# Mixture of experts behind attention: tokens fetched by indirect DMA instead of one-hot products

## The chip, the cores and the metric

The kernel runs on one core of a Trainium2 chip. The time is the device time of one execution, in microseconds (us); the figure given for a kernel is the median of its runs. Inside the core there are five engines with their own queues: TensorE (PE, with its weight loads shown as PEld), VectorE (DVE), ScalarE (ACT), GpSimd (POOL) and SyncE (SP, which here issues DMAs). They wait for one another through semaphores only.

## The reference

One pre-norm layer on x of 16 batches, 256 tokens, 128 features, all float32.

```
x = x + attention(layernorm(x))            # 16 heads, key width 8, value width 64, causal
n = layernorm(x)
probs = softmax(n @ gate_w)                # 8 experts
top_p, top_idx = top_k(probs per expert and batch, 64)      # each expert takes 64 of the 256 tokens
xin = n[top_idx]                           # (batch, expert, 64, 128)
h = gelu(xin @ w1[expert])                 # 128 -> 512
y = (h @ w2[expert]) * top_p               # 512 -> 128
x = x + scatter_add(y at top_idx)
```

## The kernel before

**Attention (lines 83 to 692).** One block. Every engine walks the same schedule of batches and, in each batch, of four units (four heads each); later stages of a batch run one to three batches behind the first. The second layer norm of batch b - 2 is made by DVE in unit 0 of batch b (`norm(xn2, ...)`, line 507) into one buffer xn2, which PE transposes in unit 1 for the gate product (line 614). In unit 1 ACT also copies xn2 to `xg_hi` (line 434, rounded to the matmul type float32r), and in unit 2 DVE writes `xg_lo`, what the rounding left (line 530). Both are kept for all 16 batches. SP stores and reloads q and k through DRAM for each batch (from line 257), loads w1 at batch 4 and w2 near the end.

**Routing (lines 871 to 911).** A second block begins when every engine has left the first. DVE makes the softmax, PE transposes it so that a row is one pair of batch and expert, and DVE finds the 64 largest of 256 in eight rounds. `tok_row` (the indices as bfloat16) goes to DRAM and comes back spread over all partitions, two batches to a load (`toks`, line 805). The indices and the probabilities are also transposed into `slot_tok` and `slot_prob`: partition = slot of an expert pair, column = batch. Meanwhile ACT and POOL split w1 into w1_hi and w1_lo (lines 838, 823).

**Experts (from line 941 on DVE, 991 on PE).** The loop `for n in STEPS` runs over -4 to 17. A step n is one pair of experts (n mod 4) for one group of four batches (n // 4), so 16 steps have products. In its step each engine does, in this order:

- PE: the pick of batch n + 4, the h products of step n (24 products: two halves of two experts, each as hi x hi, hi x lo, lo x hi), the out product of batch n - 5, the y products of step n - 1 (64 products).
- DVE: `picks(n + 5)`, which compares `toks` with the token numbers and gives a one-hot matrix; the copy of `xin_lo`; `add_out(n - 5)`, which adds two halves of the out product to x_all; `placing(n - 3)`, four one-hot matrices that put the slots back to token rows; the scaling of y by the probabilities.
- ACT: the copy of `xin_hi`, four Gelus with the rounded copy of y (`split_y`, step n - 2) between the second and the third.
- POOL: the low part of y (line 828), one pass for each step.

A pick is four products of 512 columns: xg_hi and xg_lo of a batch's two token blocks, each times the one-hot matrix. It gives the 64 tokens of all eight experts, feature by slot, so that four picks serve four steps; four of them stand ahead of the first h product. Out products of the last four batches stand behind the loop and write where the picks wrote; `last_place` reuses the pick matrices.

What the prediction's steps touch: lines 434 and 530 (xg), 507 (xn2 and its wait), 800 to 805 (the trip of the indices), 823 and 828 (POOL), 852 and 947 (xin), 863 (Gelu), 909 (slots), 926 (places), 977 (out), 999 (pick), 1018 to 1020 (h), 1035 (y).

Of the kernel before, what the change touches and what calls it, by code (L numbers as in the profile page):

```python
# [5 lines left out]
F32 = mybir.dt.float32  # L6
# [47 lines left out]
def block_kernel(nc, x, w_q, w_k, w_v, w_o, gate_w, w1, w2, out):  # L54
# [3 lines left out]
    with ExitStack() as ctx:  # L58
        def sb(name, shape, dt=F32, scope=ctx):
            return scope.enter_context(nc.sbuf_tensor(name, shape, dt))  # L60

        def sem(name, scope=ctx):
            return scope.enter_context(nc.semaphore(name))


        x_all = sb("x_all", [P, B * TB, D])
        xg_hi = sb("xg_hi", [P, B * TB, D], F32R)
        xg_lo = sb("xg_lo", [P, B * TB, D], F32R)
# [6 lines left out]
        experts_loaded = sem("experts_loaded")  # L75

        attention(nc, x_tiles, w_q, w_k, w_v, w_o, gate_w, w1, w2,
                  x_all, xg_hi, xg_lo, gate_logit, ident, w1_raw, w2_sb, k_diag_even, experts_loaded)
        experts(nc, out_tiles, x_all, xg_hi, xg_lo, gate_logit, ident, w1_raw, w2_sb,
                experts_loaded)  # L80


def attention(nc, x_tiles, w_q, w_k, w_v, w_o, gate_w, w1, w2,
              x_all, xg_hi, xg_lo, gate_logit, ident, w1_raw, w2_sb, k_diag_even, experts_loaded):
# [4 lines left out]
    with ExitStack() as ctx:  # L89
# [118 lines left out]
        xg_hi_done = sem("xg_hi_done")  # L208
        xg_lo_done = sem("xg_lo_done")
# [28 lines left out]
        def _(sp):  # L238
# [127 lines left out]
        def _(act):  # L366
# [23 lines left out]
            def batch(b, par):  # L390
                for j in range(G):
# [40 lines left out]
                    if j == 1 and has(b - 2, B):  # L432
                        act.wait_ge(xn2_ready, b - 1)
                        nc.scalar.activation(xg_hi[:, bass.ds((b - 2) * TB, TB), :], xn2[:, :, :],
                                             ACT.Copy).then_inc(xg_hi_done, 1)
# [4 lines left out]
        def _(dve):  # L440
# [26 lines left out]
            def batch(b, par):  # L467
                for j in range(G):
# [58 lines left out]
                    if j == 2 and has(b - 2, B):  # L527
                        dve.wait_ge(xg_hi_done, b - 1)
                        tiles = bass.ds((b - 2) * TB, TB)
                        nc.vector.tensor_tensor(xg_lo[:, tiles, :], xn2[:, :, :], f32(xg_hi[:, tiles, :]),  # L530
                                                ALU.subtract).then_inc(xg_lo_done, 1)
# [164 lines left out]
def experts(nc, out_tiles, x_all, xg_hi, xg_lo, gate_logit, ident, w1_raw, w2_sb, experts_loaded):  # L696
# [5 lines left out]
    with ExitStack() as ctx:  # L702
# [6 lines left out]
        def sem(name):  # L709
# [5 lines left out]
        LB = 2  # L715
        LOADS = B // LB
        STEPS = range(-4, B + 2)
# [12 lines left out]
        tok_row = sb("tok_row", [P, CAP], BF16)  # L730
# [4 lines left out]
        tok_no = sb("tok_no", [P, TB])  # L735
        col_no = sb("col_no", [P, T], BF16)
        toks = [sb(f"toks{r}", [P, LB, E * CAP], BF16) for r in range(RING)]
        pick = [sb(f"pick{r}", [P, TB, E * CAP], F32R) for r in range(RING)]
        xin_hi = [sb(f"xin_hi{r}", [P, E, QB, CAP], F32R) for r in range(RING)]
        xin_lo = [sb(f"xin_lo{r}", [P, E, QB, CAP], F32R) for r in range(RING)]  # L740
# [4 lines left out]
        place = [sb(f"place{r}", [P, EP, T], F32R) for r in range(RING)]  # L745
        tok_rows = nc.dram_tensor("tok_rows", [P, CAP], BF16).ap()

        pick_hi_ps = [ps(f"pick_hi_ps{r}", [P, E, CAP]) for r in range(RING)]
        pick_lo_ps = [ps(f"pick_lo_ps{r}", [P, E, CAP]) for r in range(RING)]
# [3 lines left out]
        last_place = [part[:, :, :].rearrange("p t (a n) -> p (t a) n", a=2) for part in pick]  # L753
        last_out_ps = [to[:, :, :].rearrange("p (t a e) s -> p t a (e s)", t=TB, a=2)
                       for to in (*pick_hi_ps, *pick_lo_ps)]

        def out_ps_of(b):

            return out_ps[:, :, :, :] if b < LAST else last_out_ps[b - LAST]

        def place_of(b):

            return place[b % RING][:, :, :] if b < B - RING else last_place[b % RING]
# [7 lines left out]
        row_ready = sem("row_ready")  # L771
        row_stored = sem("row_stored")
        toks_loaded = [sem(f"toks_loaded{i}") for i in range(LOADS)]
# [5 lines left out]
        pick_ready = sem("pick_ready")  # L779
        pick_done = sem("pick_done")  # L780
# [17 lines left out]
        def _(sp):  # L798
            sp.wait_ge(row_ready, 1)
            sp.dma_start(tok_rows, tok_row[:, :]).then_inc(row_stored, 16)  # L800
            sp.wait_ge(row_stored, 16)
            rows = tok_rows.rearrange("(b e) s -> b (e s)", e=E)
            for i in range(LOADS):
                await_count(sp, pick_ready, (i - 1) * LB)
                sp.dma_start(toks[i % RING][:, :, :],
                             bcast(rows[i * LB:(i + 1) * LB, :], 0, P)).then_inc(toks_loaded[i], 16)
# [6 lines left out]
        def _(pool):  # L813
            nc.gpsimd.iota(tok_no[:, :], pattern=[[P, TB]], base=0, channel_multiplier=1,
# [5 lines left out]
            for ep in range(EP):  # L820
# [3 lines left out]
                                        ALU.subtract).then_inc(w1_ready, 1)  # L824
            for m in range(B):
# [3 lines left out]
                                        f32(parts[:, :, m % EP, 0, :]), ALU.subtract).then_inc(y_lo_ready, 1)  # L829

        @block.scalar
        def _(act):
# [14 lines left out]
            for n in STEPS:  # L847
                b = n + 4
                if has(b, B):
                    act.wait_ge(pick_done, b + 1)  # L850
                    await_count(act, h_done, (b // QB - 1) * 16)
                    nc.scalar.activation(xin_hi[b // QB % RING][:, :, b % QB, :], pick_hi_ps[b % RING][:, :, :],  # L852
                                         ACT.Copy).then_inc(xin_hi_ready, 1)
# [11 lines left out]
                elif has(m, B):  # L865
                    split_y(m)

        @block.vector
        def _(dve):
# [30 lines left out]
            nc.vector.tensor_copy(tok_row[:, :], at).then_inc(row_ready, 1)  # L900
# [10 lines left out]

            def picks(b):

                if has(b, B):
                    if b % LB == 0:
                        dve.wait_ge(toks_loaded[b // LB], 16)
                    await_count(dve, pick_done, b - 1)
                    for tb in range(TB):
                        last = nc.vector.tensor_scalar(pick[b % RING][:, tb, :], toks[b // LB % RING][:, b % LB, :],  # L919
                                                       tok_no[:, tb:tb + 1], None, ALU.is_equal)  # L920
                    last.then_inc(pick_ready, 1)
# [18 lines left out]
            picks(0)  # L940
            for n in STEPS:
                picks(n + 5)
                b = n + 4
                if has(b, B):
                    dve.wait_ge(pick_done, b + 1)
                    await_count(dve, h_done, (b // QB - 1) * 16)
                    nc.vector.tensor_copy(xin_lo[b // QB % RING][:, :, b % QB, :], pick_lo_ps[b % RING][:, :, :]).then_inc(xin_lo_ready, 1)
# [8 lines left out]
                if B - RING <= b < B:  # L956
                    dve.wait_ge(pick_done, B)
                    placing(b)
                m = n - 1
# [12 lines left out]
        def _(pe):  # L972
# [18 lines left out]
            for n in STEPS:  # L991
                b = n + 4
                if has(b, B):
                    pe.wait_ge(pick_ready, b + 1)
                    await_count(pe, xin_hi_ready, b - 1)
                    await_count(pe, xin_lo_ready, b - 1)
                    for part, to in ((xg_hi, pick_hi_ps[b % RING]), (xg_lo, pick_lo_ps[b % RING])):
                        for tb in range(TB):
                            last = nc.tensor.matmul(to[:, :, :], part[:, b * TB + tb, :], pick[b % RING][:, tb, :],  # L999
                                                    start=(tb == 0), stop=(tb == TB - 1))  # L1000
                    last.then_inc(pick_done, 1)
                if has(n, B):
# [4 lines left out]
                    quarter = n // QB  # L1007
                    pe.wait_ge(xin_hi_ready, (quarter + 1) * QB)
                    pe.wait_ge(xin_lo_ready, (quarter + 1) * QB)
                    for k in range(4):  # L1010
                        e = 2 * (n % EP) + k // 2
                        await_count(pe, h_ready, 4 * n + k - 1)
                        for c in range(2):
                            hidden = slice((2 * (k % 2) + c) * P, (2 * (k % 2) + c + 1) * P)
                            xh = xin_hi[quarter % RING][:, e, :, :].rearrange("p b s -> p (b s)")
# [54 lines left out]
```

## Time and profile before

| | |
|---|---|
| median of 3 runs | 591.7 us (591.56 to 592.28) |
| profiled execution | 592.4 us |
| its span | 590.7 us |
| mean granted clock of TensorE | 0.976 of full speed |
| PE busy | 533.6 us, 90% |
| DVE, ACT, POOL busy | 403.1, 403.0, 252.3 us |
| DMA | 45.82 MB |

The span is the time from the first to the last instruction in the profile; 1.7 us of the profiled execution lie around it. Busy times overlap one another. Matmuls are pipelined: one is shown for longer than the distance to the next, so that the distance between starts says what a product costs in a row. The granted clock is a share of 2.4 GHz.

### The profile page before, as it was taken

Reading aid. Unit: us, or ns where it says so; the run is one execution under the profiler, and the core shown is the slowest. Engines: PE = TensorE matmul, PEld = TensorE weight load, DVE = VectorE, ACT = ScalarE, POOL = GpSimd, SP = SyncE. Lnnn points to the kernel's source line nnn. Section 1 sums busy time; section 2 is a strip of 40 time slices with the busy share of each in tenths; the row PEclk is TensorE's granted clock in tenths of the full one; section 3 lists DMA queues with packets and bytes.
Section 4 is the critical chain, followed back from the end, with each engine's and each line's share of the span. In section 5 each row is a group of like instructions: output and inputs, shape, how many; then the busy total and the mean of one; then the engine's idle time right before and its main releaser. Section 6 shows DMA issues by size and latency. Waiting matters only on the chain. (4 is left out here: it accounts for less than half of the span.)

```text
span 590.7 us, 14103 instructions
## 1 busy us (share of the span) xinstructions
PE 533.6 (90%) x4773; PEld 429.9 (73%) x4773; DVE 403.1 (68%) x1014; ACT 403.0 (68%) x1378; POOL 252.3 (43%) x245
## 2 busy tenths in 40 slices
PE   1599999999999999999999999997059999999996
PEld 1367777777777777777777777776038989989895
DVE  1477888888888888888888887874863234433344
ACT  4698988989889889888888898971215443243230
POOL 4155565555565555555655555560600110110111
PEclk9999999999999999999999999999569999999999
DMA  4585142652251431522513315500020001000001
GB/s 116 159 221 146 33 121 74 214 144 71 74 142 32 110 98 44 142 71 71 143 40 102 112 33 140 144 1 1 1 67 24 20 19 37 20 11 19 19 20 46
DMA packets 49739, 45.82 MB, mean 78 GB/s; under 512 B 4256, under 2 KB 46496, under 8 KB 49696
## 3 DMA queue, kind: packets, MB, share of 16 engines
q1 hardware_dynamic: 48832, 44.60, 27.6%
q10 hardware_dynamic: 864, 0.66, 0.4%
q8 instruction: 26, 0.43, 0.3%
q14 instruction: 17, 0.14, 0.1%
HBM read 26.35 MB, written 18.89 MB: 77 GB/s over the span
## 5 line engine op out<-in xcount | busy, mean ns | idle before, releaser
L385 ACT ACTIVATE prob<-s_ps,neg_max 128x128 f32<-128x128 f32 (+1 forms) x512 | 210.2, 437 | 21.7 <-DVE neg_max L542 20.1
L358 POOL TENSOR_TENSOR probn<-prob,inv 128x1024 f32<-128x1024 f32 x64 | 121.2, 1894 | 45.6 <-DVE inv L546 45.6
L385 ACT ACTIVATION_READ_ACCUMULATOR prob<-s_ps,neg_max 128x1 f32 x512 | 113.9, 223 | 0.0
L351 POOL TENSOR_TENSOR probn<-prob,inv 128x512 f32<-128x512 f32 x64 | 66.6, 1041 | 87.7 <-PE t_ps L659 79.3
L637 PE MATMUL ctx_ps<-probT,v_sb 128*64 128x256 f32 (+1 forms) x1024 | 97.3, 332 | 0.6 <-issue 0.6
L637 PEld LDWEIGHTS ctx_ps<-probT,v_sb 128*64 128x64 f32 x1024 | 63.5, 136 | 27.7 <-issue 9.1
L828 POOL TENSOR_TENSOR y_parts<-y_sb,y_parts 128x512 fp32r<-128x512 f32 x16 | 20.5, 1284 | 137.1 <-ACT y_parts L844 137.1
L473 DVE TENSOR_REDUCE neg_max<-s_ps 128x4 f32<-128x1024 f32 x64 | 76.5, 1196 | 1.3 <-PE s_ps L575 1.3
L650 PE MATMUL misc_ps<-wo_sb,ctxT 128*128 128x128 f32 x512 | 73.9, 288 | 0.0
L650 PEld LDWEIGHTS misc_ps<-wo_sb,ctxT 128*128 128x128 f32 x512 | 61.9, 191 | 10.8 <-issue 10.8
L599 PE MATMUL t_ps<-ident,probn 128*128 128x128 f32 x256 | 62.9, 286 | 1.0 <-ACT probT L423 0.7
L600 PE MATMUL t_ps<-ident,probn 128*128 128x128 f32 x256 | 60.2, 275 | 0.0
L1035 PE MATMUL y_ps<-w_sb,w_raw 128*64 128x128 f32 x1024 | 59.4, 274 | 0.0
L539 DVE COPY probT<-t_ps 128x512 f32<-128x512 f32 x64 | 44.2, 690 | 21.6 <-PE t_ps L659 21.5
L852 ACT ACTIVATE xin_hi<-pick_hi_ps 128x512 fp32r<-128x512 f32 x16 | 9.6, 599 | 71.9 <-PE pick_lo_ps L999 71.9
L542 DVE TENSOR_REDUCE neg_max<-s_ps 128x4 f32<-128x512 f32 x64 | 44.3, 692 | 19.1 <-PE s_ps L690 18.9
L1035 PEld LDWEIGHTS y_ps<-w_sb,w_raw 128*64 128x64 f32 x1024 | 55.6, 137 | 2.1
L863 ACT ACTIVATE w_raw<-h_ps 128x512 f32<-128x512 f32 x64 | 38.2, 599 | 26.0 <-PE h_ps L1020 23.7
L430 ACT ACTIVATE v_sb<-misc_ps 128x512 f32<-128x512 f32 x64 | 38.3, 599 | 24.7 <-PE misc_ps L557 23.7
L535 DVE COPY ctxT<-ctx_ps 128x512 f32<-128x512 f32 x64 | 43.6, 682 | 4.8 <-PE ctx_ps L637 4.8
L485 DVE CAST s_ps<-causal 128x512 f32<-128x512 bf16 x63 | 42.4, 674 | 0.0
L423 ACT ACTIVATE probT<-t_ps 128x512 f32<-128x512 f32 x64 | 41.5, 648 | 0.4 <-PE t_ps L600 0.4
(146 smaller groups left out, 1044.5 us busy)
## 6 DMA issues: line engine op xcount, KB each, us to landing
qT<-q_rows SPq DMA_DIRECT2D x15, 512.0 KB, 4.0
q_rows<-qk_hi SPq DMA_DIRECT2D x32, 128.0 KB, 2.4
q_rows<-qk_lo SPq DMA_DIRECT2D x32, 128.0 KB, 2.4
k_diag_odd<-k_rows SPq DMA_DIRECT2D x32, 128.0 KB, 4.3
k_rows<-qk_hi SPq DMA_DIRECT2D x30, 128.0 KB, 2.4
k_rows<-qk_lo SPq DMA_DIRECT2D x30, 128.0 KB, 2.4
k_diag_even<-k_rows SPq DMA_DIRECT2D x28, 128.0 KB, 4.3
w_raw<-in_L_ffn_w SPq DMA_DIRECT2D x1, 2048.0 KB, 10.4
```

Of the source, the lines that this page charges most:

```text
L351: nc.gpsimd.tensor_tensor(probn[r][:, 0:HG * P].rearrange("p (i k) -> p i k", i=HG), prob[r][:, 0:HG * P].rearrange("p (i k) -> p i k", i=HG),
L358: nc.gpsimd.tensor_tensor(probn[r][:, HG * P:].rearrange("p (i k) -> p i k", i=HG), prob[r][:, HG * P:].rearrange("p (i k) -> p i k", i=HG ...
L385: last = nc.scalar.activation(prob[r][:, first + i * keys:first + (i + 1) * keys], scores[:, i, :], ACT.Exp, bias=neg_max[:, r, block_, i: ...
L473: nc.vector.tensor_reduce(out=neg_max[:, r1, 1, :], in_=s1_ps[:, :, :], axis=AX.X, op=ALU.max, negate=True).then_inc(max1, 1)
L535: nc.vector.tensor_copy(ctxT[r2][:, :, :], ctx_ps[:, :, :]).then_inc(ctx_ready, 1)
L539: nc.vector.tensor_copy(probT[rm][:, 1024:1536], t_ps[rm][:, :]).then_inc(t_dve, 1)
L542: nc.vector.tensor_reduce(out=neg_max[:, r2, 0, :], in_=s0_ps[:, :, :], axis=AX.X, op=ALU.max, negate=True).then_inc(max0, 1)
L599: nc.tensor.transpose(t[:, i, 0:P], q0[:, 2 * f + i, :], ident[:, :])
L600: last = nc.tensor.transpose(t[:, i, P:T], q1[:, 2 * f + i, 0:P], ident[:, :])
L637: last = nc.tensor.matmul(ctx_ps[half * DV:(half + 1) * DV, pair, kb * P:T], v_sb[vb][:, kb, h * DV:(h + 1) * DV], rhs, start=(kb == 0), s ...
L650: last = nc.tensor.matmul(misc_ps[1][:, tb * D:(tb + 1) * D], ctxT[rm][:, c, tb * P:(tb + 1) * P], wo_sb[:, 2 * g + c, :], start=(g == 0 a ...
L1035: last = nc.tensor.matmul(y_ps[half * CAP:(half + 1) * CAP, q, :], hT[m % RING][:, half, c, q * CAP:(q + 1) * CAP], w2_sb[:, 2 * (m % EP) ...
```

## The change

The one-hot pick is replaced by a fetch from DRAM. In attention SP stores xn2 of each batch to a DRAM tensor `xn2_rows` (256 rows of 512 bytes a batch), and DVE waits for that store before it overwrites xn2; xg_hi and xg_lo are gone. The trip of the indices is gone as well. In its place DVE adds the batch's first row number to slot_tok (`slot_row`, unsigned integers), and POOL issues, for each step, four indirect DMAs, one for each batch of the group: row p of the buffer `xs` gets the DRAM row whose number stands in partition p of `slot_row`. There are five such buffers, so five steps are issued ahead, and from then on four gathers follow each low part of y. PE transposes the four 128 x 128 blocks of a step into one PSUM bank (`xin_ps`), one step ahead, behind the h and out products and ahead of the y products. ACT copies it to xin_hi; DVE then writes xin_lo as the difference, which needs xin_hi first. The loop starts at -1 instead of -4.

```
     sync, attention
+    def store_tokens(b):
+        sp.wait_ge(xn2_ready, b + 1)
+        sp.dma_start(xn2_rows[b * T:(b + 1) * T, :].rearrange("(t p) d -> p t d", p=P),
+                     xn2[:, :, :]).then_inc(xn2_stored, 16)
     for b in range(B):
+        if b >= 4:
+            store_tokens(b - 4)
...
+    store_tokens(B - 4)
     sp.wait_ge(s1_done, G * (B - 1))
     (load of w2)
+    for b in range(B - 3, B):
+        store_tokens(b)
+    sp.wait_ge(xn2_stored, 16 * B)
     scalar, attention
-    if j == 1 and has(b - 2, B):
-        act.wait_ge(xn2_ready, b - 1)
-        nc.scalar.activation(xg_hi[:, bass.ds((b - 2) * TB, TB), :], xn2[:, :, :], ACT.Copy)...
     vector, attention
-    await_count(dve, xg_lo_done, b - 2)
+    await_count(dve, xn2_stored, (b - 2) * 16)
...
-    if j == 2 and has(b - 2, B):
-        (xg_lo = xn2 - xg_hi)
     sync, experts
-    (tok_row to DRAM, toks back, eight loads)
     gpsimd, experts
+    def gathers(n):
+        if has(n, B):
+            await_count(pool, xin_done, n - GATHERS + 1)
+            for q in range(QB):
+                b = n // QB * QB + q
+                nc.gpsimd.indirect_dma_start(
+                    xs[n % GATHERS][:, q, :], None, xn2_rows,
+                    bass.IndirectOffsetOnAxis(ap=slot_row[:, n % EP, b:b + 1], axis=0)
+                ).then_inc(gathered[n % GATHERS], 16)
+    pool.wait_ge(xn2_stored, 16 * B)
+    pool.wait_ge(rows_ready, 1)
+    for n in range(GATHERS):
+        gathers(n)
     for m in range(B):
         (low part of y)
+        gathers(m + GATHERS)
     scalar, experts, at the end of step n
+    w = n + 1
+    if has(w, B):
+        act.wait_ge(xin_done, w + 1)
+        await_count(act, h_done, 4 * (w - 1))
+        nc.scalar.activation(xin_hi[w % RING], xin_ps, ACT.Copy).then_inc(xin_hi_ready, 1)
     vector, experts
-    nc.vector.tensor_copy(tok_row[:, :], at).then_inc(row_ready, 1)
...
+    dve.wait_ge(slots_ready, 2)
+    nc.vector.tensor_tensor(slot_row, slot_tok, row_base, ALU.add).then_inc(rows_ready, 1)
...
-    (picks, and the copy of xin_lo at the head of the step)
+    behind add_out and placing, ahead of the scaling of y:
+    dve.wait_ge(xin_hi_ready, w + 1)
+    nc.vector.tensor_tensor(xin_lo[w % RING], xin_ps, f32(xin_hi[w % RING]), ALU.subtract)...
     tensor, experts
-    (four products of 512 columns at the head of the step)
...
+    behind the out product, ahead of the y products:
+    pe.wait_ge(gathered[w % GATHERS], 16 * QB * (w // GATHERS + 1))
+    await_count(pe, xin_lo_ready, w)
+    for q in range(QB):
+        last = nc.tensor.transpose(xin_ps[:, q, :], xs[w % GATHERS][:, q, :], ident[:, :])
+    last.then_inc(xin_done, 1)
```

The places of the last two batches get two buffers of their own, and the out products of the last four batches three banks of their own and xin_ps.

## Rows read from the trace of the kernel before

**Rows 1.** The page, part 1: busy us (share of span), instructions.

```profile
PE 533.6 (90%) x4773; PEld 429.9 (73%) x4773; DVE 403.1 (68%) x1014; ACT 403.0 (68%) x1378; POOL 252.3 (43%) x245
```

**Rows 2.** Windows: length, busy us of each engine, clock, DMA share, GB/s.

```profile
414.00:430.00 16.00, 0.69 (x2) 0.29 (x2) 13.48 (x47) 4.20 (x5) 9.71 (x6) 0.50 0.00 1
...
435.60:440.20 4.60, 4.51 (x10) 3.23 (x11) 3.00 (x8) 1.20 (x2) 0.00 (x0) 0.52 0.17 57
```

**Rows 3.** Timeline, attention: start, us, engine, line, tiles, count.

```profile
246.39 1.28 PEld L637 LDWEIGHTS ctx_ps<-probT,v_sb 128*64 128x64 f32 x16 [0.17 <-issue]
...
250.66 0.41 ACT L434 ACTIVATE xg_hi<-xn 128x256 f32 x1
...
252.09 1.28 PEld L637 LDWEIGHTS ctx_ps<-probT,v_sb 128*64 128x64 f32 x16 [0.17 <-issue]
```

**Rows 4.** The page, DMA issues: count, KB each, us to landing.

```profile
out<-x_all SPq DMA_DIRECT2D x16, 128.0 KB, 1.8
...
x_all<-in_L_attn_x SPq DMA_DIRECT2D x1, 128.0 KB, 2.6
```

**Rows 5.** Timeline, the last us of attention.

```profile
411.06 0.60 DVE L455 TENSOR_SCALAR xn<-x_all,mv,rstd 128x128 f32<-128x128 f32 x2 [1.08 <-POOL rstd L346]
...
413.88 0.17 DVE L510 COPY gate_logit<-misc_ps 128x16 f32<-128x16 f32 x1 [0.79 <-PE misc_ps L606]
```

**Rows 6.** Timeline of DVE, the slots.

```profile
430.02 0.22 DVE L901 CAST tok_twice<-top_at 128x128 f32<-128x128 uint32 x1
...
431.66 0.47 DVE L909 COPY slot_prob<-h_ps 64x64 f32<-64x64 f32 x2
```

**Rows 7.** Timeline, first h products and the Gelu table.

```profile
443.47 0.28 PE L1018 MATMUL h_ps<-xin_hi,w_hi 128*128 128x256 f32 x1
...
444.42 1.28 ACT L863 ACT_TABLE_LOAD   x1
...
456.68 0.28 PE L1018 MATMUL h_ps<-xin_hi,w_hi 128*128 128x256 f32 x1
```

**Rows 8.** The page, costliest groups: busy us, mean ns, idle before.

```profile
L358 POOL TENSOR_TENSOR probn<-prob,inv 128x1024 f32<-128x1024 f32 x64 | 121.2, 1894 | 45.6 <-DVE inv L546 45.6
...
L828 POOL TENSOR_TENSOR y_parts<-y_sb,y_parts 128x512 fp32r<-128x512 f32 x16 | 20.5, 1284 | 137.1 <-ACT y_parts L844 137.1
```

**Rows 9.** Timeline, four loads issued by SP.

```profile
102.83 1.93 SPq L249 DMA_DIRECT2D k_diag_even<-k_rows  x4
```

**Rows 10.** One line's products, low and full clock (timeline of PE).

```profile
39.12 0.63 PE L690 MATMUL s_ps<-k_diag_even,qT 128*128 128x512 f32 x1
...
44.52 0.40 PE L690 MATMUL s_ps<-k_diag_odd,qT 128*128 128x512 f32 x1
```

**Rows 11.** Chain of waits: start us, us, what.

```profile
531.10 3.65 PE y_ps L1035 x64
...
539.94 3.65 PE y_ps L1035 x64
...
547.88 3.64 PE y_ps L1035 x64
```

**Rows 12.** Timeline of PE, four transposes.

```profile
403.77 0.60 PE L659 MATMUL t_ps<-ident,probn 128*128 128x128 f32 x4
404.21 0.38 PE L614 MATMUL misc_ps<-ident,xn 128*128 128x128 f32 x2
```

**Rows 13.** Timeline, DVE beside the out product.

```profile
538.83 1.11 PE L977 MATMUL out_ps<-y_parts,place 128*128 128x256 f32 x8
...
540.78 1.13 DVE L926 TENSOR_SCALAR place<-col_no,slot_tok 128x256 fp32r<-128x256 bf16 x4
```

**Rows 14.** Timeline, an out product and what it waited for.

```profile
484.59 1.19 PE L977 MATMUL out_ps<-y_parts,place 128*128 128x256 f32 x8 [0.93 <-POOL y_parts L828]
```

**Rows 15.** Timeline, POOL and DVE at once.

```profile
577.93 1.27 POOL L828 TENSOR_TENSOR y_parts<-y_sb,y_parts 128x512 fp32r<-128x512 f32 x1 [5.29 <-ACT y_parts L844]
...
578.43 1.70 DVE L926 TENSOR_SCALAR place<-col_no,slot_tok 128x256 fp32r<-128x256 bf16 x4
```

More of the change, by code:

```diff
@@ L693, in _, with experts @@
             batches(pe, batch)
-def experts(nc, out_tiles, x_all, xg_hi, xg_lo, gate_logit, ident, w1_raw, w2_sb, experts_loaded):
+def experts(nc, out_tiles, x_all, xn2_rows, gate_logit, ident, w1_raw, w2_sb, experts_loaded, xn2_stored):
     with ExitStack() as ctx:
@@ L714, in experts @@
         QB = 4
-        LB = 2
-        LOADS = B // LB
-        STEPS = range(-4, B + 2)
+        GATHERS = 5
+        STEPS = range(-1, B + 2)
         LAST = B - QB
@@ L734, in experts @@
         slot_prob = sb("slot_prob", [P, EP, B])
-        tok_no = sb("tok_no", [P, TB])
+        row_base = sb("row_base", [P, EP, B])
+        slot_row = sb("slot_row", [P, EP, B], U32)
         col_no = sb("col_no", [P, T], BF16)
[L737 to L740, printed above, removed]
+        xs = [sb(f"xs{r}", [P, QB, D]) for r in range(GATHERS)]
+        xin_hi = [sb(f"xin_hi{r}", [P, 2, QB, CAP], F32R) for r in range(RING)]
+        xin_lo = [sb(f"xin_lo{r}", [P, 2, QB, CAP], F32R) for r in range(RING)]
         hT = [w1_raw[:, r * EP:(r + 1) * EP, :].rearrange("p (h a) (k n) -> p h (a k) n", h=2, n=QB * CAP)
@@ L744, in experts @@
         y_parts = [sb(f"y_parts{r}", [P, QB, EP, 2, D], F32R) for r in range(RING)]
[L745 to L749, printed above, removed]
+        place = [sb(f"place{r}", [P, EP, T], F32R) for r in range(2 * RING)]
+        xin_ps = ps("xin_ps", [P, QB, 2 * CAP])
         h_ps = [ps(f"h_ps{r}", [P, 2, QB * CAP]) for r in range(RING)]
@@ L752, in experts @@
         out_ps = ps("out_ps", [P, TB, 2, D])
-        last_place = [part[:, :, :].rearrange("p t (a n) -> p (t a) n", a=2) for part in pick]
-        last_out_ps = [to[:, :, :].rearrange("p (t a e) s -> p t a (e s)", t=TB, a=2)
-                       for to in (*pick_hi_ps, *pick_lo_ps)]
+        last_ps = [ps(f"last_ps{i}", [P, TB, 2, D]) for i in range(QB - 1)]
         def out_ps_of(b):
-            return out_ps[:, :, :, :] if b < LAST else last_out_ps[b - LAST]
+            if b < LAST:
+                return out_ps[:, :, :, :]
+            if b < B - 1:
+                return last_ps[b - LAST][:, :, :, :]
+            return xin_ps[:, :, :].rearrange("p (t a) d -> p t a d", t=TB)
         def place_of(b):
-            return place[b % RING][:, :, :] if b < B - RING else last_place[b % RING]
+            return place[b % RING if b < B - RING else b % RING + RING][:, :, :]
         numbered = sem("numbered")
@@ L770, in experts @@
         found = sem("found")
-        row_ready = sem("row_ready")
-        row_stored = sem("row_stored")
-        toks_loaded = [sem(f"toks_loaded{i}") for i in range(LOADS)]
+        rows_ready = sem("rows_ready")
+        gathered = [sem(f"gathered{r}") for r in range(GATHERS)]
         twice_ready = sem("twice_ready")
@@ L798, in _ @@
         def _(sp):
[L799 to L806, printed above, removed]
             with sp.Fori(0, B) as b:
@@ L847, in _ @@
             for n in STEPS:
[L848 to L853, printed above, removed]
                 m = n - 2
@@ L910, in _ @@
             dve.wait_ge(numbered, 2)
[L912 to L921, printed above, removed]
+            dve.wait_ge(slots_ready, 2)
+            nc.vector.tensor_tensor(slot_row[:, :, :], slot_tok[:, :, :], row_base[:, :, :], ALU.add).then_inc(rows_ready, 1)
             def placing(b):
@@ L956, in _ @@
                 if B - RING <= b < B:
-                    dve.wait_ge(pick_done, B)
                     placing(b)
+                w = n + 1
+                if has(w, B):
+                    dve.wait_ge(xin_hi_ready, w + 1)
+                    await_count(dve, h_done, 4 * (w - 1))
+                    nc.vector.tensor_tensor(xin_lo[w % RING][:, :, :, :], xin_ps[:, :, :].rearrange("p b (h s) -> p h b s", h=2),
+                                            f32(xin_hi[w % RING][:, :, :, :]), ALU.subtract).then_inc(xin_lo_ready, 1)
                 m = n - 1
@@ L991, in _ @@
             for n in STEPS:
[L992 to L1001, printed above, removed]
                 if has(n, B):
```

47 lines of the change are left out of this document (17 added, 30 removed).

## The prediction

> **What bounds the kernel now.** First the page's busy shares: PE is busy 90% of the span, the next engine 68% [rows 1]. Then windows along the span: attention ends at about 414 us; in the routing, from 414 to 430 us, PE works 0.69 us and its granted clock is 0.50, which is 1.2 GHz, while DVE is busy 13.48 of 16 [rows 2]; behind it come the experts, where PE is the limit again, as its share says. So an edit counts only where it changes what PE does, or what PE waits for around routing.
>
> Attention is not moved by what ACT and DVE do beside it. The unit that holds the xg_hi copy runs from ctx product to ctx product in 5.70 us (246.39 to 252.09), with PE's weight loads idle 0.17 at its end, for an issue and not for ACT [rows 3]. Taking 16 ACT copies (0.41 us) and 16 DVE subtractions out is worth 0; if PE did wait for ACT, the most is 16 x 0.41 = 6.6.
>
> **The change, part by part.** The sum is made against the profiled execution: 592.4 us, of which 590.7 is span; 1.7 lies around it. The median of the runs is 591.7, 0.7 below; I carry the difference over to the median.
>
> *The stores of xn2.* 16 stores of 128 KB enter SP's queue. Each stands ahead of SP's wait for the next batch's qk_hi, and DVE waits for it a batch (four units, some 23 us) later; the same 128 KB land in 1.8 (out) to 2.6 us (x) [rows 4]. Cover is ample, cost 0; without it each would cost its 2 us. Only the last one is naked: xn2 of batch 15 is ready at 411.66, the store lands at 413.5 to 414.3, and the engines now leave the block when DVE's last copy ends, 414.05 [rows 5]. 0 to +0.25; I take 0.1.
>
> *Routing to the first h.* Before, the indices are repeated from 430.02, the slots are finished at 432.13 [rows 6], and the first h product, behind a trip of the indices to DRAM and four picks, starts at 443.47 [rows 7]. After: one cast of about 0.1 us less ahead of this, one small addition more (0.2, like its neighbours), so POOL may begin at about 432.3; its four w1 low parts are done by then. Then four gathers for step 0, each 128 rows of 512 B.
>
> No row shows a DMA issued by POOL. Bounds for one: above, 1.89 us, POOL's pass over 128x1024, with 1.28 for 128x512 between [rows 8]; below, 0.48 us, SP's four k_diag issues in 1.93 [rows 9]. A gather has a quarter of the 1.28 row's bytes but an address to work out for each row, so I take 1.1, near that row. Landing: 1.8 to 2.6 us [rows 4]; I take 2.0. The Trainium skill, "DMA: Bandwidth & Descriptors", section on the SWDGE path, puts about 2.0 us plus bytes/436e3 on a whole POOL-issued DMA, which would give 2.15 for 64 KB; no run so far shows it.
>
> Rows for step 0 have landed at 432.3 + 4.4 + 2.0 = 438.7. Four transposes at the low clock 0.9 (twice their 0.44 below), xin_hi 0.6, xin_lo 0.69 that now must follow xin_hi, and three hand-overs of 0.1: h(0) begins at 441.2, 2.3 us earlier than before.
>
> But PE comes cold. Before, the picks kept it busy 4.51 of the 4.60 us from 435.6 to 440.2, at a clock of 0.52 [rows 2], and the h products behind that ran at 2.4 GHz. Now h(0) is its first real work, and it is broken: 12 products of 0.213 (256 columns at 1.2 GHz), then the wait for the Gelu table (1.28) and the first Gelu (0.6), which stood there before too [rows 7], then 12 more, then T(1), then a pause while ACT copies xin_hi(1) and DVE makes xin_lo(1), since no y product stands behind it yet. The kernel's own start shows how long the low level can last where the work has pauses: the same 512-column product takes 0.63 us at 39.12 and 0.40 at 44.52 [rows 10]. So I take h(0) and most of h(1) at 1.2 GHz. h(0): 2.6 + 0.75 + 2.6 ends at 447.2; its last Gelu at 448.0, xin_hi 448.6, xin_lo 449.35; h(1) begins at 449.4. I let the clock come back as late in h(1) as it did behind the first pick, so h(1) takes 4.9 where 3.3 would do, to 454.3; T(2) 0.43, y(0) 3.65: h(2) begins at 458.4. Before it began at 456.68 [rows 7]. The lead of 2.3 has become a debt of 1.7.
>
> *The steady steps.* Before, a step with picks lasts 8.84 us (531.10 to 539.94), one without 7.94 (539.94 to 547.88): the picks cost 0.90 [rows 11]. Four transposes of 128x128 cost 0.44 in a row (403.77 to 404.21) [rows 12]; I take 0.43. Steps 2 to 11 lose picks and gain transposes: 10 x (0.90 - 0.43) = 4.7 saved. Steps 12 to 14 had no picks and now carry transposes: 3 x 0.43 = 1.3 lost. Net 3.4 saved.
>
> What hides the new chain in a step: transposes end 1.6 us after the out product's start, ACT's last Gelu at about +0.8, so xin_hi at 2.2. DVE starts the places at +1.95 and ends them at +3.1, xin_lo at +3.8 [rows 13]; h(n+1) starts behind out (1.04), T (0.43) and y (3.65) at +5.1 [rows 11]. Slack 1.3 us. For the last two places (+1.05) it still holds.
>
> *POOL.* Its queue holds 20 gathers before the low part of y(0), then y_lo(m) and four gathers by turns. The first reader that hurts is the out product of step 5, which wants y_lo(3): POOL gets there at 432.3 + 32 x 1.1 + 4 x 1.28 = 472.6; PE gets there at 458.4 + 3 x 7.43 + 3.26 = 484.0 (steps of 8.37 less out's 0.95, then h). Before, that product waited 0.93 for y_lo itself [rows 14]; this stays in steps 5, 9 and 13, on both sides. In the steady part POOL needs 4.4 + 1.28 = 5.7 of 8.37 us. xs has five buffers: gathers for step m+5 are issued in step m+2, two steps ahead of use.
>
> The tail behind y(15) is untouched. Sum: 0.1 + 1.7 - 3.4 = -1.6: **590.1 us** (profiled 590.8). The likeliest case's own range is 588.5 to 591.7.
>
> **The rivals.**
>
> *A. POOL becomes the bound (slower).* The price per gather decides. y_lo(3) arrives in time up to 432.3 + 32c + 5.1 = 484.0 + 0.9, c = 1.48. At c = 1.6 it comes at 488.6, where the out product before stood at 484.59: +4.0, less 7 x 0.47 = 3.3 and plus 1.3: +2.0, 593.7. At the upper bound 1.89 it is 497.9, and POOL's step of 8.84 exceeds PE's 8.37: y_lo(11) at 568.6 against an out product at 555.7, +12.9 and 0.9 for the last transposes: 605.5. For it: 64 gathers are the largest block of work added anywhere, on an engine whose every row is slow. Against: POOL stands idle 137 us before its 16 low parts (20.5 busy) [rows 8], and five buffers give it a long start.
>
> *B. DVE and POOL collide (slower).* When POOL ran y_lo at 577.93, DVE's four places took 1.70 instead of 1.13 us [rows 15]: one place waited for POOL's instruction. The gathers start when y_lo ends, at about out +1.0, right over the places (+1.9 to +3.1). If a gather holds its port as y_lo does, each of the four places can wait for one: 4.4 for 1.13, 3.3 more, less the slack of 1.3 = 2.0 per step, over eight or nine steps +17: 607. If DVE wins each time, POOL loses 1.1 us a step and has 2.7 to spare: 0. Against: a gather reads one column of indices, where y_lo streams 128x512 twice. The Trainium skill, "SBUF — State Buffer", "Who interferes with whom", says that a VectorE instruction in a two-port mode and a GpSimd instruction exclude each other for the whole instruction; its section "SBUF: two separate sides" adds that the making of DMA descriptors on GpSimd starves in that case. Of the two, the 1.70 agrees for a compute instruction, and nothing here shows it for a gather. By that rule taken fully the time is that of B or 0, by who is first.
>
> *C. The start goes well (faster).* Gathers at 0.48: 2.5 us earlier. Clock back before h(1): 1.6 more. Together -5.7, 586.0; either alone 587.6 or 588.5.
>
> *D. It does not help because the start eats all.* Gathers at 1.3 to 1.45, POOL still in time: 0.8 to 1.4 later, and a cold y(0) of up to 1.8 more: 590.9 to 593.
>
> **How the numbers follow.** Forecast 0.42; A 0.16; B 0.08; C 0.16; D 0.18. A change under 0.2% (1.2 us) can't be told from none. Faster: C, and three quarters of the forecast (0.32): 0.48. Same (590.5 to 592.9): the rest of the forecast and half of D: 0.19. Slower: A, B and the other half of D: 0.33. Range: down to 586.0, all of C; up to 599, A to c = 1.75 (POOL at 493.5, +7); only B and the far end of A are outside.
>
> **What would show it.** Right: gathers on POOL about 1.1 apart from 432.3; rows landed at 438.7; first h at 441.2 with products 0.213 apart; h(2) near 458.4; steps of 8.4 us from then on; y_lo(3) ready before step 5 ends. Wrong: an out product or y_sb that waits for POOL (A); places over 0.35 us with xin_lo late and PE waiting at h (B); steps of 0.115 already in h(0) (C); attention's end moved from 414.4, or units in attention no longer 5.70; transposes over 0.5 us in the experts.

## The result: 622.3 us, 5.1% slower

The median went from 591.63 us (4 runs, 590.03 to 592.28) to **622.33 us** (4 runs, 619.76 to 622.62), ratio 1.051, 95% interval 1.048 to 1.055. The forecast was 590.1, its range 586 to 599, with 0.48 on faster: wrong in sign, and the time is outside the range. The profiled execution took 622.62 us, span 620.9, granted clock 0.959.

The page of the changed kernel: busy times, the costliest groups that the change touches (busy us, mean ns | idle before, its largest releaser), and one row of the DMA issues (count, KB, us to landing).

```profile
PE 536.9 (86%) x4773; PEld 431.3 (69%) x4773; DVE 385.3 (62%) x966; ACT 396.8 (64%) x1362; POOL 313.9 (51%) x309
...
L820 POOL DMA_INDIRECT xs<-xn_rows,slot_row x64 | 61.3, 957 | 24.3 <-issue 16.2
...
L1023 PEld LDWEIGHTS y_ps<-w_sb,w_raw 128*64 128x64 f32 x1024 | 57.4, 137 | 16.0 <-issue 15.7
...
L831 POOL TENSOR_TENSOR y_parts<-y_sb,y_parts 128x512 fp32r<-128x512 f32 x16 | 20.5, 1284 | 81.8 <-ACT y_parts L848 81.8
...
xn_rows<-xn SPq DMA_DIRECT2D x16, 128.0 KB, 4.2
```

PE is as busy as before in microseconds (536.9 against 533.6), on a span that is 30.2 longer [rows 1]: it does no more, it stands more. No engine has become the bound: POOL is at 51% and still waits 81.8 us for ACT before its low parts. What is new is idle time in front of the y products that is put down to "issue", that is, to nothing that the profile shows.

In what follows h(n), y(n) and T(n) are the h products, the y products and the four transposes of step n. Where the 30 us lie can be read from three marks: DVE's first operation of the routing (`neg_top`), the start of y(0), the start of y(14). The first mark stands at 414.33, before at 414.38, so attention shows no change. From one profile to another this mark moves by up to 3 us (411.37 to 414.38, with or without the change; only experiment 10, which loads attention, stands apart), so every kernel is counted from its own mark. The tails behind y(14) are equal (18.0).

| us | mark to y(0) | y(0) to y(14) | mark to end |
|---|---|---|---|
| before | 37.6 | 120.7 | 176.3 |
| after | 50.5 | 138.0 | 206.6 |
| difference | +12.9 | +17.3 | +30.2 |

**The start.** Timeline of the changed kernel (start, us, engine, line, tiles, count, [idle before and its releaser]).

```profile
433.12 1.22 POOL L820 DMA_INDIRECT xs<-xn_rows,slot_row  x1 [6.79 <-DVE slot_row L915]
...
437.14 0.94 POOL L820 DMA_INDIRECT xs<-xn_rows,slot_row  x1 [0.30 <-issue]
...
439.75 1.11 PE L1014 MATMUL xin_ps<-ident,xs 128*128 128x128 f32 x4 [8.78 <-DMA xs<-xn_rows,slot_row]
...
442.37 0.55 PE L999 MATMUL h_ps<-xin_hi,w_hi 128*128 128x256 f32 x1 [1.50 <-DVE xin_lo L949]
...
447.90 0.60 ACT L861 ACTIVATE w_raw<-h_ps 128x512 f32<-128x512 f32 x1 [1.45 <-PE h_ps L1001]
...
448.74 1.05 PE L1014 MATMUL xin_ps<-ident,xs 128*128 128x128 f32 x4
...
452.87 0.60 ACT L861 ACTIVATE w_raw<-h_ps 128x512 f32<-128x512 f32 x1 [4.37 <-remote]
...
457.14 0.60 ACT L869 ACTIVATE xin_hi<-xin_ps 128x512 fp32r<-128x512 f32 x1 [3.67 <-remote]
457.77 0.69 DVE L949 TENSOR_TENSOR xin_lo<-xin_ps,xin_hi 128x512 fp32r<-128x512 f32 x1 [15.55 <-issue]
...
458.71 0.55 PE L999 MATMUL h_ps<-xin_hi,w_hi 128*128 128x256 f32 x1 [8.92 <-issue]
```

Up to 448 us it goes nearly as forecast. Then h(0) is finished (448.94) and T(1) too (448.74 + 1.05 = 449.8), so ACT should have all that the last Gelu and xin_hi(1) need, and yet the Gelu starts at 452.87 and xin_hi at 457.14. No producer is named for either ("remote"), but the trace also holds the time of each semaphore increment: PE's increment for the end of h(0) stands at 452.85, that for T(1) at 457.12. ACT starts 0.02 us behind each. So what is late is PE's signal, 3.9 and 7.3 us behind the end that the trace gives its products (these ends are modelled, the starts and the increments are recorded), and ACT and DVE only follow. PE begins h(1) at 458.71, when the 20th gather has ended (458.05).

**A steady step.** The same view, one step.

```profile
511.54 0.96 POOL L820 DMA_INDIRECT xs<-xn_rows,slot_row  x1 [0.16 <-issue]
...
511.90 3.63 PE L1023 MATMUL y_ps<-w_sb,w_raw 128*64 128x128 f32 x56
...
512.37 1.13 DVE L920 TENSOR_SCALAR place<-col_no,slot_tok 128x256 fp32r<-128x256 bf16 x4
...
512.80 1.00 POOL L820 DMA_INDIRECT xs<-xn_rows,slot_row  x1 [0.30 <-issue]
...
515.35 0.94 POOL L820 DMA_INDIRECT xs<-xn_rows,slot_row  x1 [0.30 <-issue]
...
515.83 0.49 PE L1023 MATMUL y_ps<-w_sb,w_raw 128*64 128x128 f32 x5 [0.30 <-issue]
...
517.27 0.44 PE L1023 MATMUL y_ps<-w_sb,w_raw 128*64 128x128 f32 x3 [0.96 <-issue]
...
517.75 0.69 DVE L958 TENSOR_TENSOR y_sb<-y_ps,slot_prob 128x512 f32<-128x512 f32 x1 [3.65 <-PE y_ps L1023]
...
586.55 3.71 PE L1023 MATMUL y_ps<-w_sb,w_raw 128*64 128x128 f32 x64
...
594.94 3.71 PE L1023 MATMUL y_ps<-w_sb,w_raw 128*64 128x128 f32 x64
```

The 64 y products of a step wait for nothing among themselves. Beside four gathers in a row (511.54 to 516.29) they break after some 56, start again twice, and take 5.8 us instead of 3.7. In the last steps, which issue no gathers, they run unbroken, and a step lasts 594.94 - 586.55 = 8.39 us: the 8.37 of the forecast. With gathers a step lasts 10.4.

### The profile page after: what moved, and what is told of

Read it like the earlier page. It is cut to its first block and busy times, and to the rows that moved or that the text cites. A ratio compares the mean times of both kernels' runs of the same rounds, so it can differ in the third digit from the quotient of the medians.

```text
span 620.9 us, 14098 instructions
## 1 busy us (share of the span) xinstructions
PE 536.9 (86%) x4773; PEld 431.3 (69%) x4773; DVE 385.3 (62%) x966; ACT 396.8 (64%) x1362; POOL 313.9 (51%) x309
## 3 DMA queue, kind: packets, MB, share of 16 engines
q0 software_dynamic: 2048, 4.20, 2.7%
## 5 line engine op out<-in xcount | busy, mean ns | idle before, releaser
L820 POOL DMA_INDIRECT xs<-xn_rows,slot_row x64 | 61.3, 957 | 24.3 <-issue 16.2
L1023 PE MATMUL y_ps<-w_sb,w_raw 128*64 128x128 f32 x1024 | 65.1, 275 | 9.5 <-issue 8.9
L1023 PEld LDWEIGHTS y_ps<-w_sb,w_raw 128*64 128x64 f32 x1024 | 57.4, 137 | 16.0 <-issue 15.7
L831 POOL TENSOR_TENSOR y_parts<-y_sb,y_parts 128x512 fp32r<-128x512 f32 x16 | 20.5, 1284 | 81.8 <-ACT y_parts L848 81.8
L999 PE MATMUL h_ps<-xin_hi,w_hi 128*128 128x256 f32 x128 | 41.6, 325 | 13.4 <-issue 10.2
```

What stands on the lines that cost most here:

```text
L820: nc.gpsimd.indirect_dma_start(xs[n % GATHERS][:, q, :], None, xn2_rows, bass.IndirectOffsetOnAxis(ap=slot_row[:, n % EP, b:b + 1], axis=0 ...
L999: nc.tensor.matmul(to, w1_hi[:, e, hidden], xh, start=True, stop=False)
L1023: last = nc.tensor.matmul(y_ps[half * CAP:(half + 1) * CAP, q, :], hT[m % RING][:, half, c, q * CAP:(q + 1) * CAP], w2_sb[:, 2 * (m % EP) ...
```

## The experiments

The theory after the trace (G): indirect DMAs issued by POOL in a long run hold the other engines up. Its rivals: any DMA from POOL's queue does it (Q); the bytes into SBUF do it (M); it is the new order of transposes and copies (O). From experiment 5 on the expectations split G in two: theory B (only a run of gathers costs) and theory P (each gather costs its share). Medians beside are those of the kernel before from the same chip and time.

**1 and 2: the same order, plain loads.** Both leave out the choice of rows: each load takes the first 128 rows of its batch. In the first SP issues them, behind the same counts (its loop of output stores is unrolled for it, and holds the loads of step b + 10 behind store b); in the second POOL does, and the edit is only this:

```
-                        nc.gpsimd.indirect_dma_start(
-                            xs[n % GATHERS][:, q, :], None, xn2_rows,
-                            bass.IndirectOffsetOnAxis(ap=slot_row[:, n % EP, b:b + 1], axis=0)).then_inc(...)
+                        nc.gpsimd.dma_start(xs[n % GATHERS][:, q, :],
+                                            xn2_rows[b * T:b * T + P, :]).then_inc(...)
```

> The changed kernel with its gathers replaced by plain loads of the same size, issued by SP: the first 128 rows of each batch instead of the chosen ones (the choice of rows is left out, everything else stays: order, buffers, waits). The changed kernel has steps of 10.4 us where I forecast 8.4, and a start with 9 us of idle PE. Theory G (the gathers themselves hold the other engines up while POOL issues them): no such stalls, steps of 8.4, first h near 441, 588 to 591 us. Theory O (the new order transposes, xin_hi, xin_lo costs the time): steps stay at 10.4 and the total near 622.

> As the run with SP's loads, but the plain loads stay on POOL's queue, in the gathers' places (the choice of rows is left out). If it is the indirection (an address for each row) that holds the others up: near 590. If it is any DMA whose descriptors POOL makes: near 622, steps near 10.4. Theory O: near 622 as well, but then the run with SP's loads is too.

Measured: 586.57 us from SP, 587.67 us from POOL, beside 590.51: ratios 0.994 both (0.992 to 0.996; 0.992 to 0.996). Both are somewhat faster than expected. The order is not to blame (O is out), and neither are DMAs from POOL's queue as such (Q is out): the page counts 2048 packets and 4.20 MB on that queue in the second run and in the changed kernel alike. Timeline of the second:

```profile
431.03 9.22 POOL L820 DMA_DIRECT2D xs<-xn_rows  x17 [6.50 <-DVE slot_row L914]
...
435.00 1.11 PE L1013 MATMUL xin_ps<-ident,xs 128*128 128x128 f32 x4 [5.83 <-DMA xs<-xn_rows]
...
437.62 0.55 PE L998 MATMUL h_ps<-xin_hi,w_hi 128*128 128x256 f32 x1 [1.50 <-DVE xin_lo L948]
...
449.78 0.40 PE L1000 MATMUL h_ps<-xin_hi,w_lo 128*128 128x256 f32 x1
449.99 0.30 PE L998 MATMUL h_ps<-xin_hi,w_hi 128*128 128x256 f32 x1
...
451.62 3.71 PE L1022 MATMUL y_ps<-w_sb,w_raw 128*64 128x128 f32 x64
```

17 plain DMAs take 9.22 us, 0.54 each (all 20 ahead of the loop take 10.80), against 1.25 from one gather's start to the next. The rows also show the cold start that the forecast had assumed: products of h(0) and of most of h(1) 0.21 apart, at the lower of the two levels of the clock, until 449.99, in h(1), where it comes back to 2.4 GHz.

**3: gathers that nobody reads, in the kernel before.** After each of the first 11 low parts of y, POOL issues four gathers of x rows into free tiles:

```
+                if m < 11:
+                    await_count(pool, dead_landed, 16 * 4 * m)
+                    for q in range(4):
+                        nc.gpsimd.indirect_dma_start(dead[q], None, dead_src,
+                            bass.IndirectOffsetOnAxis(ap=dead_at[:, :], axis=0)).then_inc(dead_landed, 16)
```

> The kernel before, with four gathers of 128 rows of 512 B behind each of the first 11 low parts of y, into tiles that nobody reads; nothing waits for them but the next four and POOL's end. Theory G: about 2 us more in each step that has them, 11 x 2 = 22 us, 605 to 616 us, with PE pauses inside the y products. Theory O: 591 to 592, since no engine but POOL has anything new.

Measured: 610.91 us beside 590.51, ratio 1.036 (1.031 to 1.042): +20.4, without transposes, without stores, with the old picks. The first such run in its timeline:

```profile
458.76 3.71 PE L1050 MATMUL y_ps<-w_sb,w_raw 128*64 128x128 f32 x64
459.90 1.23 POOL L841 DMA_INDIRECT left<-in_L_attn_x,dead_at  x1 [0.18 <-issue]
...
464.31 0.69 DVE L981 TENSOR_TENSOR y_sb<-y_ps,slot_prob 128x512 f32<-128x512 f32 x1 [7.53 <-remote]
...
465.76 0.60 ACT L867 ACTIVATE xin_hi<-pick_hi_ps 128x512 fp32r<-128x512 f32 x1 [6.30 <-remote]
```

By the modelled ends y(1) is complete at 462.47, yet DVE scales it at 464.31; the pick is complete by 463.6, yet ACT copies it at 465.76. The recorded increments say what "remote" hides: PE's for y(1) stands at 464.29, its one for the pick at 465.74, and DVE and ACT start 0.02 us behind them. From 432 us on, 16 of PE's 112 increments in this run come 0.7 to 3.0 us behind the end of their product; in the kernel before and in the plain version of experiment 2 none is more than 0.03 behind. No recorded increment of DVE, ACT or POOL is late here, and neither DVE nor ACT starts more than 0.03 us behind the increment that it waits for. So a run of gathers holds up PE, in its starts and in its signals, and DVE and ACT wait for PE.

**4: rows of 128 bytes.** The gathers of the change fetch 32 columns instead of 128 (and the wrong ones, so the values that the experts work on are not the tokens'; POOL first fills the buffers with zeros, which is left out below):

```
-                            xs[n % GATHERS][:, q, :], None, xn2_rows,
+                            xs[n % GATHERS][:, q, 0:32], None, xn2_rows.rearrange("r (k c) -> (r k) c", c=32),
```

> The changed kernel with gathers of 128 B rows instead of 512 B (a quarter of the bytes, as many rows and gathers; the wrong columns are fetched). If the making of the descriptors is what hurts: as the changed kernel, 615 to 623. If it is the data on the DMA engines: most of it goes, 595 to 605.

Measured: 624.38 us beside 590.51, ratio 1.056 (1.052 to 1.060). A quarter of the bytes changes nothing (M is out), and not the price of a gather either; its row on the page:

```profile
L821 POOL DMA_INDIRECT xs<-xn_rows,slot_row x64 | 61.2, 956 | 22.0 <-issue 16.8
```

**5 and 6: the change with a shorter lead, spread or in runs.** Both issue the gathers of two steps ahead of the loop (8 in place of 20) and those of step n + 2 in step n. In the first the four are spread behind four different waits:

```
+                    pool.wait_ge(h_done, 4 * n + 2)
+                    gather(n + 2, 0)
                     ...                                 # low part of y(n - 2)
+                    gather(n + 2, 1)
+                    pool.wait_ge(xin_done, n + 2)
+                    gather(n + 2, 2)
+                    await_count(pool, y_done, n)
+                    gather(n + 2, 3)
```

In the second all four stand behind the low part of y and a wait for h_done, 4n + 4.

> The changed kernel, complete, with its 64 gathers spread: eight ahead of the loop, then in step n one each behind the second h product group, behind the low part of y, behind the transposes and behind the y products, for step n + 2. Theory B (what hurts is a run of gathers: the other engines have some us of work in hand, and stop only when that is used up): the pauses go, steps of 8.4, only the eight at the start still cost, 588 to 596. Theory P (each gather costs the others its share whenever it comes, about 0.5 us): steps stay near 10.4, about 612 to 620.

> The same lead of two steps and the same eight gathers ahead of the loop, but the four gathers of a step stand in one run behind the low part of y and the h products. Theory B: steps of 10 us as in the changed kernel, the start better than there (no 9 us of idle PE), 605 to 615, and so 12 us or more over the spread one. Theory P: the same as the spread one within 2 us.

Measured: spread 591.96 us (10 runs) beside 591.22, ratio 1.001 (0.999 to 1.003); in runs of four 610.72 us, ratio 1.032 (1.028 to 1.036). Same gathers, same products, same lead: the difference of 18.8 is how closely they follow one another. Theory B holds and P falls. The spread one, chain of waits (start, us, what), then POOL in the same stretch:

```profile
493.48 0.96 PE out_ps L979 x8
...
494.88 3.64 PE y_ps L1033 x64
...
501.88 0.95 PE out_ps L979 x8
```

```profile
492.04 0.95 POOL L819 DMA_INDIRECT xs<-xn_rows,slot_row  x1 [0.66 <-PE h_ps L1011]
493.00 1.31 POOL L836 TENSOR_TENSOR y_parts<-y_sb,y_parts 128x512 fp32r<-128x512 f32 x1
494.46 0.96 POOL L819 DMA_INDIRECT xs<-xn_rows,slot_row  x1 [0.16 <-issue]
495.73 0.98 POOL L819 DMA_INDIRECT xs<-xn_rows,slot_row  x1 [0.31 <-issue]
498.81 0.95 POOL L819 DMA_INDIRECT xs<-xn_rows,slot_row  x1 [2.10 <-PE y_ps L1033]
```

The y products are unbroken and the step is 8.40. In runs of four the same line breaks as in the changed kernel:

```profile
515.35 0.52 PE L1028 MATMUL y_ps<-w_sb,w_raw 128*64 128x128 f32 x5 [0.20 <-issue]
516.80 0.31 PE L1028 MATMUL y_ps<-w_sb,w_raw 128*64 128x128 f32 x1 [0.93 <-issue]
```

**7 to 9: how many in a row.** The edit of experiment 3 with one, two and three gathers in place of four.

> The kernel before, with one unused gather behind each of the first 11 low parts of y, where four cost 20.4 us (611 against 590.5). Theory B: nothing, 590.5 within 1. Theory P: a quarter, 5 us, 595.6.

> The kernel before, with two unused gathers behind each of the first 11 low parts of y; one cost nothing (590.9 against 591.2), four cost 20 us. If the other engines have a few us in hand and stop only beyond that: 591 to 593. If the cost grows evenly from the second on (20 us for three more): 598.

> Three in a run instead of two. With some us in hand: the run lasts 3.6 us, and PE's pauses began 3.5 us behind the first of four; so a small cost, 592 to 600, and most of the 20 us comes with the fourth. Evenly from the second on: 604.

| gathers in a row, 11 times | median us | ratio to the kernel before (interval) | per run of gathers |
|---|---|---|---|
| 1 | 590.89 | 0.9996 (0.9985 to 1.0008) | 0 |
| 2 | 590.82 | 0.9995 (0.9983 to 1.0006) | 0 |
| 3 | 597.66 | 1.0115 (1.0097 to 1.0134) | 0.6 us |
| 4 | 610.91 | 1.036 (1.031 to 1.042) | 1.9 us |

In a row one gather follows the other by 1.25 us in all of them, so the cost is not proportional to POOL's time: two are free, the third costs 0.6, the fourth 1.3, its full length. Three cost less than the even growth that would have given 604. Chain of waits, three in a row (gathers at 493.48, 494.75, 496.06), and two in a row:

```profile
493.50 3.31 PE y_ps L1050 x57
496.81 0.14 issue
496.95 0.54 PE y_ps L1050 x5
497.49 0.19 issue
497.68 0.38 PE y_ps L1050 x2
```

```profile
494.10 3.64 PE y_ps L1050 x64
```

**10: one unused gather per unit of attention, in the kernel before.**

```
                             bcast(inv[:, r, 1, :], 2, T), ALU.mult).then_inc(normed, 1)
+                        nc.gpsimd.indirect_dma_start(
+                            dead[:, :], None, dead_src,
+                            bass.IndirectOffsetOnAxis(ap=dead_at[:, :], axis=0)).then_inc(dead_landed, 16)
```

> The kernel before, with one unused gather in each of the 64 units of attention, on POOL behind its second normalisation, and none in the experts. POOL has room: 3.1 of 5.8 us busy. If single gathers are free (theory B) and the loop of attention fares no worse than the unrolled experts: 590 to 592. Theory P: 64 x 0.5 = 32 us, 622. A third outcome, POOL's products late by 1.25 us on the way to the transposes, would show as PE waiting for POOL: up to 64 x 1 us.

Measured: 640.35 us beside 591.22, ratio 1.080 (1.074 to 1.087). None of its three forecasts is met, and it says nothing on G: I had let the next normalisation wait for the gather's landing (`dead_landed`), and POOL's waits for it add up to more than the 49 us that were lost. Its waits (engine, line, waited for: us in total, times, longest):

```profile
POOL probn L359 <- DMA dead<-in_L_attn_Wv,dead_at: 78.3, 43, 3.7
```

It does show that in attention, unlike in the experts, POOL has no room for a gather and its landing.

**11 and 12: the cold start.** Products that nobody reads, on w1 and into y_ps, ahead of the first transposes of the spread kernel (26) or the first pick of the kernel before (12):

```
+            pe.wait_ge(w1_ready, 1)
+            for i in range(26):
+                nc.tensor.matmul(y_ps[:, :, :].rearrange("p q d -> p (q d)"), w1_hi[:, 0, 0:P], w1_hi[:, 1, :],
+                                 start=True, stop=True)
```

> The complete changed kernel with its gathers spread (592.0), and 26 products of 512 columns, whose result is overwritten, on PE between the slot transposes and the first transposes of rows, where it stands idle 8.7 us. Theory W (my step of the cold start): h(0) and h(1), 24 products each, then run at 0.107 to 0.115 instead of 0.213, 2.6 + 1.7 us less: 587 to 588.5, below the kernel before. Rival: the start is bound by the gathers, the Gelu table and the way T, xin_hi, xin_lo, and the faster products only wait: 591 to 592.

> The kernel before with 12 such products ahead of its first pick, where PE stands idle 4.6 us. It shows how much of a gain of the warmed, spread kernel belongs to the warming and not to the change. Theory W: the eight picks and picks' products that ran at 0.43 now run at 0.22, but DVE's pick matrices (0.9 us each batch) and the copies bound them soon: 0.5 to 2 us less, 589 to 590.5. Rival: 591 to 592.

Measured, 12 runs each, beside 591.19: spread and warm 589.14 us, ratio 0.9974 (0.9961 to 0.9987), between theory W and its rival; before and warm 590.01 us, ratio 0.9979 (0.9968 to 0.9990), as theory W had it. PE's timeline, the spread kernel with 26 products, and its window from 439 to 441 us (last three numbers: granted clock, DMA share, GB/s):

```profile
427.68 8.07 PE L995 MATMUL y_ps<-w_hi 128*128 128x512 f32 x26
436.78 0.66 PE L1028 MATMUL xin_ps<-ident,xs 128*128 128x128 f32 x4 [1.04 <-DMA xs<-xn_rows,slot_row]
...
439.51 0.41 PE L1015 MATMUL h_ps<-xin_hi,w_lo 128*128 128x256 f32 x1
...
442.82 0.28 PE L1014 MATMUL h_ps<-xin_lo,w_hi 128*128 128x256 f32 x1
```

```profile
439.00:441.00 2.00, 2.00 (x9) 2.00 (x10) 0.00 (x0) 0.35 (x1) 0.94 (x1) 0.50 0.20 59
```

The transposes take 0.66 where cold ones took 1.11 (at 435.00 in experiment 2). Behind two waits of PE, 1.04 and 1.51 us, the first half of h(0) is at 1.2 GHz again (clock 0.50), so that 12 x 0.1 us of the gain that theory W had counted on did not come; but the second half is at 2.4 already, and all of h(1). Spread and warm is the fastest complete version, and it is faster than before, by 0.3%. Of its 2.0 us the kernel before gets 1.2 from warming alone; the 0.9 left between the two warm versions is within their scatter (587.89 to 591.82 and 587.91 to 591.17), so that the indirect fetch itself is worth anything is not shown.

## Why the prediction was wrong

The marks of the runs that decide, from one profile each:

| us | mark to y(0) | y(0) to y(14) | mark to end |
|---|---|---|---|
| before | 37.6 | 120.7 | 176.3 |
| forecast, its prices | 40.4 | 117.3 | 175.7 |
| plain loads by POOL | 39.1 | 117.5 | 174.7 |
| gathers spread | 42.2 | 117.8 | 177.9 |
| spread, warm | 38.8 | 117.8 | 174.5 |
| four in a row, lead of two steps | 42.1 | 138.4 | 198.6 |
| after | 50.5 | 138.0 | 206.6 |
| before with unused, four in a row | 37.9 | 140.3 | 196.1 |
| before with unused, three in a row | 38.6 | 127.2 | 183.7 |

So the 30.2 of the change are 20.2 for runs of four in the steps (138.0 against 117.8), 8.4 for the run of 20 at the start (50.5 against 42.2), and 1.6 for everything else. Point by point:

- *The stores of xn2; xg taken out.* Right as far as the runs can tell: the mark is 414.33 against 414.38, but it moves by 3 us between profiles, so 0.1 can't be seen in it. In the seven profiles with these stores it lies at 411.37 to 414.33, in six without them at 411.58 to 414.38. The stores landed in 4.2 us, not in 1.8 to 2.6 [rows 4], and it did not matter.
- *Routing to the first h.* POOL began at 433.12, 0.9 behind the end of slot_row, not at 432.3. A gather costs 1.25 (0.94, and 0.30 before the next), not 1.1. From the start of the fourth to PE's transposes it is 2.6 us; I had 1.1 + 2.0. The Trainium skill, "DMA: Bandwidth & Descriptors", section on the SWDGE path, has a fit for a whole DMA of this kind; worked out for 64 KB it is an estimate of 2.15 us. The 2.6 measured here has the semaphore's way to PE in it. h(0) came at 442.37, 1.2 later than forecast, 1.1 earlier than before [rows 7].
- *PE comes cold.* Right in kind, rather too dear: in the plain version y(0) came 39.1 behind the mark. The forecast has 40.4 (h(1) ends at 454.3, T(2) 0.43, the mark at 414.38).
- *The sum.* It had a slip of one pick. Before, a pick stands between y(0) and h(2) (it starts at 455.65, h(2) at 456.68 [rows 7]), so the debt of 1.7 has been credited with it already, and ten picks were then taken out of the steps again. Counted from y(0), the debt is 2.7 (454.7 against 452.0) and the ten picks are right: the same prices give 0.1 + 2.7 - 3.4 = -0.6, not -1.6. The plain version gave +1.5 and -3.2.
- *The steady steps, and what hides the new chain.* Right for every step without a run of gathers: 8.39 against 8.37, of which T is 0.44 (a step without it lasts 7.95), places 1.13.
- ***POOL*, the step that failed.** "In the steady part POOL needs 4.4 + 1.28 = 5.7 of 8.37 us": with the measured price it is 5 + 1.3 = 6.3, which still fits. PE's one named wait for y_lo is 0.8 us, 0.9 before, so rival A fell. But a gather was priced in POOL's time alone. I asked what it costs the engine that issues it and when its rows land, and put what it costs PE at nothing, without a row that shows it. PE runs on beside two in a row; beside four it loses 1.9 us each time (experiment 3), and the 20 at the start cost 8.4 more than eight.
- *Rival B* was the only one in which a gather hurts another engine, and it had the wrong place. In the step shown above a gather runs from 511.54 and another from 512.80, and the four places, from 512.37 to 513.50, take 1.13 beside them; so do all eight sets of places that ran beside gathers in the changed kernel. In the spread kernel some take 1.20, no more. The Trainium skill, "SBUF — State Buffer", "Who interferes with whom", has a VectorE instruction in a two-port mode and a GpSimd instruction shut each other out for the whole instruction: y_lo beside the places agrees [rows 15], the steps with gathers do not show it, and it would not have stopped PE.
- *The five buffers.* They were counted as safety. They made it worse: 20 gathers in one run, 24.9 us, through the stretch in which h(0), the first Gelus and xin(1) go from engine to engine. A lead of two steps was enough.

What stays open is why. PE's breaks lie between products that wait for no semaphore, so late semaphores alone don't explain them. That PE runs short of new instructions doesn't explain the other half: in experiment 3 the pick and h products behind y(1) had started before the increment of y(1) rose. The trace also holds the loads of instructions, 26 of 16 KB on one queue before and after the change; none falls into the run of gathers from 532.46 to 537.24, and PE breaks beside it too.

What sets in looks like a count, not a time. In the eleven runs of four of the changed kernel 54 to 57 products start from the first gather on until one follows late: after 3.1 to 3.3 us in nine of them, after 4.0 and 4.1 us in the two that begin together with an out product (at 500.45 and 542.78), whose products take longer. In the start, where PE does little, the signal for the third quarter of h(0) was 0.2 us late 14.8 us after the first gather, and only the next was late by 3.9. It fits that something which PE passes on for each product piles up beside the gathers, until PE has to stop; the increments themselves it can't be, since only the last of 64 y products has one. No run tests this, and none tells whether the profiler's recording takes part, since every run on record has a recorded span.

## What to carry to other kernels

Price an indirect DMA of GpSimd twice: its own time (here 1.25 us for 128 rows, whatever their length), and what a run of them takes from a dense TensorE and from all that wait for its signals; beside a dense engine issue one or two, then let something else stand between. The deepest prefetch is not the safest: issue as few ahead as the landing (2.6 us) asks for. When a term of the sum rests on "it runs beside", ask the trace for a row in which such a thing ran beside a dense engine, and if there is none, put a price and a chance on it.

## What the runs showed of the hardware

- Indirect DMAs on POOL's queue, 128 rows each: 0.94 us, 0.30 to the next, the first 1.22; the same for 128 and 512 bytes a row. Plain ones on the same queue: 0.54, and 20 of them in a row broke nothing.
- Runs of gathers beside the experts: 0, 0, 0.6 and 1.9 us for 1, 2, 3 and 4; 8.4 for the 20 at the start against 8.
- Beside runs of four in a kernel that doesn't use them, 16 of PE's 112 semaphore increments rise 0.7 to 3.0 us behind the modelled end of their product; without gathers all rise within 0.03. DVE and ACT start within 0.03 of the increment either way.
- VectorE's four one-hot writes beside indirect DMAs: 1.13 us, as without; beside a GpSimd pass over 128x512: 1.70.
- A pause in front of the first h products costs the clock even after 26 dense products: 1.04 and 1.51 us of waiting, and the next products are 0.21 apart again, at a granted clock of 0.50.
